# Causal attention of one core: from two interleaved streams of batches to one stream of groups of four heads in pairs of PSUM banks

## What is computed

```python
h = _layernorm(x) * (1 + ca) + sa
x = x + ga * attn(h)            # attn below, for all 8 sequences
h = _layernorm(x) * (1 + cb) + sb
x = x + gb * ffn(h)             # six layers, not touched

def attn(x):
    q, k, v = x @ Wq, x @ Wk, x @ Wv           # 16 heads of 64
    logits = q k^T / 8 + causal mask           # 512 x 512 a head
    return softmax(logits) @ v @ Wo + bo
```

## Time and profile before

| | us |
|---|---|
| median of 3 runs | 4380.98 (4377.91 to 4388.51) |
| the profiled execution, its own time | 4385.59 |
| its span, first to last instruction | 4383.6 |
| causal stage, to the end of the last second layer norm | 1104.9 |
| from there to the end (six local layers) | 3278.7 |

### The profile page before, as it was taken

How to read it: one execution, slowest core, us unless ns; L and a number is a source line. 1 busy time by engine, 2 the same in 40 slices (tenths; PEclk the granted TensorE clock), 3 DMA queues, 4 the chain that set the end, 5 groups by cost and what they waited for, 6 DMA issues and landing times.

```text
span 4383.6 us, 164197 instructions
## 1 busy us (share of the span) xinstructions
PE 3959.9 (90%) x72308; PEld 2187.4 (50%) x72308; DVE 3109.0 (71%) x4053; ACT 2392.5 (55%) x3362; POOL 2347.9 (54%) x2148
## 2 busy tenths in 40 slices
PE   6878878788699999999899998999989999999996
PEld 2434434343355555555455555555555555555553
DVE  5656666665577778777677777777777777777774
ACT  3444444353456656655566556556565566565563
POOL 1434344243556656656566655566656566566651
PEclk8888788897799999999999999999999999999998
DMA  1000000000344444444344544544435444444443
GB/s 50 1 6 1 4 4 1 6 2 4 97 110 109 92 102 116 101 111 107 90 110 101 116 94 98 117 108 95 111 89 118 101 109 101 98 108 107 98 104 87
DMA packets 162077, 348.82 MB, mean 80 GB/s; under 512 B 32606, under 2 KB 41948, under 8 KB 155100
## 3 DMA queue, kind: packets, MB, share of 16 engines
q1 hardware_dynamic: 161372, 338.32, 33.0%
HBM read 24.24 MB, written 4.19 MB: 6 GB/s over the span
## 4 chain that ended last, share of the span: by engine, by line
PE 76%; DVE 9%; issue 5%; ACT 5%; DMA 3%; SPq 2%; POOL 1%; ACTq 0%; DVEq 0%; POOLq 0%
PE psB L612 31%; PE psA L612 24%; PE psB L496 6%; PE psA L496 6%; DVE top L1078 3%; PE psB L690 2%; PE psA L664 2%; DMA vev<-vo 2%; PE psB L664 2%; ACT pb L920 1%; POOL pt L1233 1%; PE psA L690 1%; ACT wk L827 1%; DVE top L1075 1%; SPq L443 1%
## 5 line engine op out<-in xcount | busy, mean ns | idle before, releaser
L1233 POOL TENSOR_TENSOR pt<-wk,pt 128x256 f16<-128x256 f32 (+3 forms) x512 | 405.5, 816 | 677.2 <-ACT pt L832 622.8
L1257 POOL TENSOR_TENSOR sq<-sq 128x512 f32<-128x512 f32 x384 | 490.1, 1296 | 476.1 <-ACT sq L890 475.9
L1252 POOL TENSOR_TENSOR h<-h,ts 128x512 f32<-128x512 f32 x384 | 490.2, 1276 | 210.6 <-DVE ts L1144 210.6
L1253 POOL TENSOR_TENSOR h<-h,ts 128x512 f32<-128x512 f32 x384 | 489.8, 1276 | 0.0
L890 ACT ACTIVATE sq<-psA 128x1024 f32<-128x1024 f32 x240 | 245.8, 1024 | 161.6 <-PE psA L612 161.6
L1085 DVE CAST pt<-wk 128x512 f16<-128x512 f32 (+3 forms) x256 | 183.7, 725 | 198.5 <-ACT wk L827 195.1
L1136 DVE TENSOR_TENSOR h<-psA,t_rot 128x1024 f32<-128x1024 f32 x240 | 292.8, 1220 | 40.6 <-ACT sq L890 18.1
L1144 DVE TENSOR_TENSOR ts<-psA,t_rot 128x1024 f32<-128x1024 f32 x240 | 291.2, 1213 | 3.1 <-POOL h L1253 3.1
L612 PE MATMUL psB<-vev,ptb 64*32 64x65 f32 x9216 | 246.0, 227 | 51.1 <-ACT pb L920 35.9
L612 PEld LDWEIGHTS psB<-vev,ptb 64*32 64x32 f32 x9216 | 195.7, 107 | 167.9 <-issue 94.8
L1152 DVE TENSOR_TENSOR h<-h,psB 128x1024 f32<-128x1024 f32 x192 | 229.5, 1216 | 45.0 <-PE psB L612 42.9
(11 more groups left out here) (302 smaller groups left out, 10917.8 us busy)
## 6 DMA issues: line engine op xcount, KB each, us to landing
qf<-h SPq DMA_DIRECT2D x768, 136.0 KB
kf<-h SPq DMA_DIRECT2D x768, 136.0 KB
vev<-vo SPq DMA_DIRECT2D x192, 260.0 KB, 4.1
vev<-vo SPq DMA_DIRECT2D x192, 227.5 KB, 4.6
stage<-wqk SPq DMA_DIRECT2D x12, 512.0 KB, 4.7
stage<-wvl SPq DMA_DIRECT2D x12, 256.0 KB, 5.2
stage<-wof SPq DMA_DIRECT2D x6, 512.0 KB, 5.2
xb<-xt SPq DMA_DIRECT2D x8, 256.0 KB, 7.2
```

Source lines behind the costliest of these rows:

```text
L1233: e.tensor_tensor(p[:, 1, o:o + w], wk[n][(2 * I + x) % SLOTS][:, 0:w], p[:, 0, o:o + w], ALU.subtract).then_inc(s_cplo[n])
L1252: e.tensor_tensor(halves_of(h, 0), halves_of(h, 0), t[1], ALU.subtract)
L1253: e.tensor_tensor(halves_of(h, 1), halves_of(h, 1), t[0], ALU.add).then_inc(ended["ad"])
L1257: e.tensor_tensor(sqb[c][:, 0, :], sqb[c][:, 0, :], sqb[c][:, 1, :], ALU.add).then_inc(ended["qa"])
```

## The change

There is one stream now. A table, `CAUSAL`, holds 93 steps, and it is walked once for each sequence and once more at the ends (`causal_walk`); a step marked `+1` is one of the next sequence. The digits behind a step's name are half, g, then i and pr (maxima) or pr and j (scores), and the letter is the PSUM ring. All five engines follow this one list. Each ring now has two tiles of 1024 float32, a pair of banks each, in place of four banks.

- A step works on a pair of banks: a projection step (`c_v`, `c_qk`) makes 1024 columns, a maxima step (`c_mx`), a score step (`c_sc`) and a value step (`c_va`) both heads of a pair, a transpose step (`c_ot`) both pairs of the group. PE's matmuls are the same ones in number and width. ACT, DVE and POOL read both banks in one instruction, so they issue about half as many, each twice as wide.
- The buffers `qk`, `vt`, `pt`, `ngm`, `top`, `oq`, `crc` are indexed by g or half and no longer by stream; `wk` has six slots of 2x512 for all.
- For pr = 0 ACT writes the high part of the probabilities itself, for pr = 1 DVE casts it. The share of each is as before.
- The layer norm is four steps: `lc`/`ec` (centre, square, copy), `lm`/`em` (mean of squares), `lr`/`er` (Ln, Exp) and `lx`/`ex` (Newton step and what follows), with steps of the current sequence between them.
- The local stage is not touched.

PE before, at a place in the middle: `psA<-xb` and `psA<-wu` are the two matmuls of the first layer norm of a new sequence, `psB<-qk1k` with `t_masks` its score maxima of the other stream, `psA<-w16l` the new sequence's first projection.

The diff, cut to its core:

```diff
+CAUSAL = (
+    "sc1103:A lc:B+1 mx1021:B sc1101:A mx1031:A lm:B+1 va001:B mx1030:A sc1113:B mx1000:A mx1020:B sc1100:B "
+    "mx1010:A va000:A lr+1 ng10:B lx+1 sc1102:A sc1112:B sc1003:A sc1010:B sc1012:B ot01:A sc1011:A sc1002:B "
+    "sc1013:A qk010:B+1 qk011:A+1 v11:B ot00:A sc1000:B mx0121:A+1 sc1001:A mx0130:B+1 va110:A va111:B mx0100:A+1 "
...
+def plan_causal(steps, rings):
+    at, had, use = [0, 0], [[0] * 2, [0] * 2], {}
+    for key, c in [("mod", 0)] + [(s, "AB".index(rings[s])) for s in steps if s in rings]:
+        i = at[c] % 2
         at[c] += 1
         use[key] = (c, i, had[c][i])
         had[c][i] += 1
...
-        pt = [[sb(f"pt{n}{i}", [128, 2, 8 * 160], F16, early) for i in range(4)] for n in range(2)]
-        wk = [[sb(f"wk{n}{i}", [128, 512], F32, early) for i in range(SLOTS)] for n in range(2)]
+        pt = [[sb(f"pt{n}{i}", [128, 2, 2, 8 * 160], F16, early) for i in range(2)] for n in range(2)]
+        wk = [sb(f"wk{i}", [128, 2, 512], F32, early) for i in range(SLOTS)]
...
 # PE
+                elif kind == "c_qk":
+                    half, g, pr = s[2:]
+                    at = 128 * (4 * half + 2 * g + pr)
+                    o = take(s)
+                    e.wait_ge(s_w16, 3)
+                    e.wait_ge(s_hl[n], k + 1)
+                    for x in range(2):
+                        p = mm3(o[:, 512 * x:512 * x + 512], [w16[z][:, x, at:at + 128] for z in range(2)],
+                                [t[:, :] for t in h16[n]])
+                    p.then_inc(full(s)[0])
...
+                elif kind == "c_ng":
+                    half, g = s[2:]
+                    o = take(s)
+                    for i, pr in MAXIMA:
+                        e.wait_ge(*freed(("c_mx", b, half, g, i, pr)))
...
+                elif kind == "c_va":
+                    half, g, pr = s[2:]
+                    o = take(s)
+                    for j in range(NT):
+                        e.wait_ge(*low(("c_sc", b, half, g, pr, j)))
+                    for u in range(2):
+                        e.wait_ge(*freed(("c_v", b, half, u)))
...
 # ACT
-                    for x in range(2):
-                        J = 16 * G(k, half, g) + 8 * pr + 2 * j + x
-                        o = bank(s + (x,))[:, 0:w]
-                        if J >= SLOTS:
-                            e.wait_ge(s_cplo[n], J - SLOTS + 1)
-                        e.wait_ge(*full(s + (x,)))
-                        p = e.activation(wk[n][J % SLOTS][:, 0:w], o, ACT.Exp, scale=0.125)
-                        if x:
-                            p.then_inc(freed(s + (x,))[0])
-                            continue
-                        p.then_inc(s_cexp[n])
-                        e.activation(pt[n][(2 * pr + x) % 4][:, 0, OFFS[j]:OFFS[j] + w], o, ACT.Exp, scale=0.125
-                                     ).then_inc(freed(s + (x,))[0])
+                    i, before = slot_of(s)
+                    if before:
+                        e.wait_ge(*low(before))
+                    e.wait_ge(*full(s))
+                    p = e.activation(wk[(i - 1) % SLOTS][:, :, 0:w], both(s, w), ACT.Exp, scale=0.125)
+                    if pr:
+                        p.then_inc(freed(s)[0])
+                    else:
+                        e.activation(pt[g][pr][:, :, 0, OFFS[j]:OFFS[j] + w], both(s, w), ACT.Exp, scale=0.125
+                                     ).then_inc(freed(s)[0])
...
 # DVE
+                elif kind in ("c_lm", "c_em"):
+                    e.wait_ge(*full(s))
+                    e.tensor_scalar(acc[n][:, :], side(s, 0), 1e-5, None, ALU.add).then_inc(freed(s)[0])
+                elif kind in ("c_lx", "c_ex"):
                     e.wait_ge(s_lnr[n], m + 1)
                     newton(acc[n][:, :], wq, wt, s_lnn[n], 5 * m)
...
-                    e.wait_ge(*freed(s + (1,)))
-                    e.tensor_copy(pt[n][2 * pr + 1][:, 0, OFFS[j]:OFFS[j] + w], wk[n][J % SLOTS][:, 0:w]).then_inc(s_cphv[n])
+                    if pr:
+                        e.wait_ge(*freed(s))
+                        e.tensor_copy(pt[g][pr][:, :, 0, OFFS[j]:OFFS[j] + w], wk[(slot_of(s)[0] - 1) % SLOTS][:, :, 0:w]
+                                      ).then_inc(s_cphv[g])
...
 # POOL
+                if pr:
+                    e.wait_ge(s_cphv[g], turn(s, 3, 4))
+                else:
+                    e.wait_ge(*freed(s))
+                e.tensor_tensor(pt[g][pr][:, :, 1, o:o + w], wk[(slot_of(s)[0] - 1) % SLOTS][:, :, 0:w],
+                                pt[g][pr][:, :, 0, o:o + w], ALU.subtract).then_inc(s_cplo[g])
```

381 lines of the change are left out of this document (167 added, 214 removed), and 6 rows, old and new, of the table CAUSAL.

## The result

| | before | changed |
|---|---|---|
| median, us | 4379.44 (4376.49 to 4388.51) | 4064.14 (4059.15 to 4072.16) |
| ratio, 95% interval | 1 | 0.928 (0.926 to 0.930) |
| profiled execution, us | 4385.59 | 4063.49 |
| end of the causal stage, us | 1104.9 | 790.8 |
| from there to the end, us | 3278.7 | 3270.6 |

The change makes the kernel 315 us faster.

The account below looks back on a forecast made before the run. PE was taken to bound the causal stage: floor 96 us plus waits and clock, 102 a sequence. 92 + 7 x 102 + 38 + 6.9 + 11.3 = 862 us, 243 less than before, so 4138 us, range 4090 to 4200.

Parts of the forecast that it names:

- The floor: PE's work for one causal sequence at full clock: 93.5 us summed by steps, 96 with turns.
- the 15.3: PE's time for score maxima in one sequence: 3.8 us a group, four groups, 15.3 us.
- the 2.4 us for turns: On PE, changes between half-array and whole-array steps at 24 score steps: about 0.1 us each, 2.4 a sequence.
- Waits and clock: PE's losses a sequence: 3.5 us waiting behind `lx` and `ex` (bounds 1.4 and 6), plus 2 for clock and gaps.
- clock and small gaps: PE's further loss in each causal sequence, taken as 2 us from the local stage's clock of 0.98.
- The ends: Causal stage outside the seven whole walks: first walk ends at 92 us; last walk 38, output product 6.9, then 11.3.
- 78% busy, 63 us: First walk of the table: 49 us of PE work at 78% busy takes 63 us, ending at 92 (85 to 102).
- PE alone: Rival: in the causal stage only PE's floor and about 1 us remain, 97 us a sequence, 4103 us; chance 0.15.
- DVE's blocks: Rival: `lx` and `ex` held 2 us each beside POOL, casts 2 ns an element; 108 a sequence, 4180 us; chance 0.13.
- The clock did not stay down: Rival: PE's causal clock stays at 0.83 from stops at tile changes; 113 us a sequence, 4215 us; chance 0.08.
- Slower: Rival: DVE's two-bank reads take twice the time an element; 140 us a sequence, 4404 us; chance 0.02.
- no effect: Rival: the order leaves PE waiting, a causal sequence keeps 133 us, only better ends remain, 4355 us; chance 0.02.

Follow-up runs that it names:

- e6: The changed kernel with the six maxima steps of each group in one run directly ahead of their transposes: 4314.6 us, ratio 0.986 to the kernel before.
- e1: The changed kernel with masks following each pair's two matmuls in maxima steps i = 0 and 1, as before the change: 4090.2 us, ratio 0.934 to the kernel before.
- e3: The changed kernel with every ACT, DVE and POOL read of two banks split into one instruction a bank: 4080.1 us, ratio 0.932 to the kernel before.
- e8: The changed kernel with masks alternately ahead of and behind half-array matmuls, and the second norm's last three instructions moved behind qk101: 4036.1 us.
- e10: The changed kernel with each group's maxima in one run and both layer norms in one piece: 4378.1 us, ratio 0.999 to the kernel before.
- e11: The changed kernel with maxima gathered in one run for two of a sequence's four groups: 4196.3 us, ratio 0.958 to the kernel before.
- e5: The kernel before with only its layer norms cut in two chunks and dealt out early: 4310.5 us, ratio 0.986 to the kernel before.
- e7: The changed kernel with the last three instructions of the second layer norm as a step behind qk101: 4053.4 us, ratio 0.926 to the kernel before.
- e12: The changed kernel with alternating mask order, the second norm's tail behind qk101, and POOL's subtraction in two instructions: 4022.0 us, ratio 0.919.
- e2: The changed kernel with each layer norm's four steps together in one piece again: 4179.8 us, ratio 0.955 to the kernel before.

## Why the prediction was wrong

The sum of the prediction against what was measured:

| | predicted | measured | difference |
|---|---|---|---|
| first walk ends at | 92 | 82.9 | -9.1 |
| seven whole walks | 714 (7 x 102) | 656.1 (7 x 93.7) | -57.9 |
| last walk to the output product | 38 | 33.4 | -4.6 |
| output product and end | 18.2 | 18.4 | +0.2 |
| end of the stage | 862 | 790.8 | -71 |
| local stage | 3278.7 | 3270.6 | -8.1 |
| profiled execution against the median | 4.6 above | 0.7 below | +5.3 |

**The floor, 96 where it is 90.3: the step that failed first.** "Its matmuls are the same as before, so nothing here can be below 93.5" is wrong: PE is busy for 90.29 us in the sequences with a clock of 1.00, and for 91.1 in the mean. Over seven walks that is 40 of the 74 us by which the forecast was too long. Four prices in the sum were off. PE's timeline of the changed kernel has them: transposed maxima, a maxima step of i = 0, one of i = 1 and the values of a pair.

```profile
335.29 0.60 PE L573 MATMUL psA<-t_mats,top 128*128 128x128 f32 x4
335.72 0.38 PE L505 MATMUL psB<-h161l,w16h 128*128 128x512 f16 x1
...
343.54 0.28 PE L505 MATMUL psA<-qk1h 64*128 64x128 f16 x4
343.76 0.40 PE L505 MATMUL psA<-t_masks 128*128 128x128 bf16 x4
344.09 0.28 PE L505 MATMUL psB<-qk0h,qk0l 64*128 64x256 f16 x2
...
347.81 0.39 PE L505 MATMUL psB<-qk1h 64*128 64x256 f16 x4
348.14 0.40 PE L505 MATMUL psB<-t_masks 128*128 128x128 bf16 x4
348.37 1.97 PE L505 MATMUL psA<-v,pt 128*128 128x65 f16 x60
350.28 0.34 PE L505 MATMUL psB<-qk1h 64*128 64x384 f16 x2
```

- Transposed maxima take 0.43 us, not 0.88. The 0.88 of the earlier trace rows was read just behind a wait of 1.58 us, in a stretch (427 to 433.7) where the clock was 0.50; e6 shows the same 0.88 at a clock of 0.50. With four a sequence that is 1.8 us.
- A maxima step of i = 0 or 1 takes 0.55 and 0.56 us, not 0.88, since its four masks follow one another. I had seen that a turn costs 0.1 and had not looked at how the new code orders the matmuls within a step. The maxima together are about 2.6 us below the 15.3, and e1, which undoes this, gives 1.6 of them back.
- Values take 1.91 us a pair (348.37 to 350.28), not 2.04: 1.0 us. The norms' matmuls take 1.01 each, not 0.87, 0.6 us the other way.
- These make 4.8 of the 5.7 us. The rest is not traced; it may lie in the 2.4 us for turns. A score step with a half-array step behind it does cost 0.1 more, but the turns as a whole fell from 128 to 112 a sequence, and a step ahead of a whole-array one is cheaper: maxima of 512 columns take 0.45 us there (344.95 to 345.40) and 0.53 elsewhere (346.41 to 346.94).

One row would have caught most of it. PE's busy time by its granted clock in the earlier trace rows is 217.83 x 0.83 = 181 us for two sequences, 90.4 for one at full clock; the sum by steps said 96, and the two were never put side by side.

**Waits and clock, 5.5 where it is 3.6.** Both blocks were named rightly and in the right order of size: 2.0 us behind `ex`, 0.8 behind `lx`, against 1.4 to 3.4 and 0 to 2. But the tile was another one. The count had PE waiting at `va001` for `mx1021`, and 0.2 us to spare at `qk100`; PE waits at `sc1111` for `qk100`. DVE, then PE:

```profile
258.36 0.68 DVE L984 TENSOR_TENSOR wu<-wu 128x512 f32<-128x512 f32 x1
...
266.70 1.22 DVE L1079 SCALAR_TENSOR_TENSOR qk0l<-psB,qk0h 128x1024 f16<-128x1024 f32 x1
```

```profile
267.97 0.34 PE L505 MATMUL psB<-qk1h,qk1l 64*128 64x384 f16 x2 [1.97 <-DVE qk0l L1079]
```

The block `ex` took 7.7 us, 258.36 to 266.06, and not the 4.7 that were taken, with two of its instructions held beside POOL. Of the further 2 us for "clock and small gaps, as the local stage's 0.98 shows" 0.8 came, at a clock of 0.99: the local stage is no measure for this one.

**The ends, 14 us.** The step "78% busy, 63 us" for the first walk had no row behind it. PE was busy for 50.95 of 53.50 us, 95%, at 0.97; the 49 us of work were nearly right, and the longest wait is 1.2 us. The last walk has 33.05 us of work up to the output product (34.4 predicted) and hardly a wait, where 3.6 us had been taken for POOL.

**What was right.** The gain lies in the causal stage alone. DVE's work falls from 83.4 to 74.1 us a sequence (74 predicted), which is luck in part: summed over the windows of two sequences, the casts' own durations fell from 22.1 to 13.7 us a sequence, not by 2, and the norms' rose from 12.8 to 16.8, which the sum left out. A double-width read of the projections takes 1216 to 1221 ns (1220), and this gain lies beside PE for the most part (e3). The waits at the layer norms vanish, and with them the low clock. A turn between half and whole array was taken at 0.1 us; e1 has 0.1 and e8 0.06.

**What was right but half told.** The prediction laid PE's holes to the layer norms, and said that the other stream "has just its maxima there". e6, e10 and e11 show that the maxima were the larger part, 30.9 us a sequence against 16.2. In the trace of before the waits for `top` were 18.2 of 48.4 us, and the low clock of the earlier trace rows began at 263, behind the first of the two waits at the norm, and lasted to 280. The sum did not need the split, as it started from PE's floor; an engineer who had cured the norms alone would have had e5's 1.4%, not 7.2%.

**The rivals.** PE alone (97 a sequence, 4103) had the mechanism, PE busy for 97% of the time, with the same wrong floor; at the right floor it would have said 91. DVE's blocks (108) were present, `ex` held for 3.0 us and `lx` for 1.6 where that rival took 2 each, but the casts took 1.3 ns an element (13.7 us for 10240), not 2, and DVE had the room. The cast of 0.23 us that the earlier trace rows has as alone ran beside POOL too (POOL's rows 446.85 to 448.43); casts of that size with POOL idle take 0.21 us, so the reading stands, but being beside POOL does not always cost. The clock did not stay down. The Trainium skill's page TensorE: Matmul & The Clock Gate, section A second HAM failure mode: psum-queue depth-cycling, spoke for that rival. In e7, e8 and e12 PE cycles through the same four tiles and the clock stays at 1.00; in the changed kernel it falls in every second sequence, right behind the wait of 2.0 us (at 269.7), and in e2, e6 and e10 it falls about waits of 1.6 to 7 us. "Slower" and "no effect" did not happen, though e10 shows how near "no effect" was: it is this change without the spread of the maxima and norms.

## What to carry to other kernels

Where one engine is to be the bound, put its busy time times its granted clock beside the sum of its steps: it is roughly the floor at full clock, and it shows at once a price that was read at half clock. It is rough because the mean clock counts idle time too: for the same matmuls it gives 90 in the two kernels here and 87 to 89 in e2, e6, e10 and e11. When an engine must answer another many times (here DVE's six maxima for one transpose), spread these steps among work that doesn't depend on them; such a hole costs its own length and, here, 0.3 (e2, 3.6 to 12.6 us) to 0.8 (the kernel before, 17.9 to 21.4) of it again in clock. Wider instructions pay only on an engine that is waited for, and on POOL they can make DVE slower.
